# A fused decoder layer on one core: key and value products move to slot 2, the next batch's query product to slot 11

## The reference

```python
def _L0_attn_ref(x, Wq, Wk, Wv):
    q = (x @ Wq.T).reshape(B, S, NH, DK).transpose(0, 2, 1, 3)
    k = x @ Wk.T
    v = x @ Wv.T
    dist = jax.nn.softmax(jnp.einsum('bhqd,bkd->bhqk', q, k) * scale, axis=-1)
    att = jnp.einsum('bhqk,bkd->bhqd', dist, v)
    return att.transpose(0, 2, 1, 3).reshape(B, S, DIM_V)
...
x = _layernorm(x + _L0_attn_ref(x, ...))
x = _layernorm(x + _L0_xattn_ref(x, ctx_1024, ctx_1024, fside_1xSxS2_0, ...))
x = _layernorm(x + _L0_ffn_ref(x, ...))
```

## Time and profile before

| | us |
|---|---|
| median of 3 runs | 1420.98 |
| lowest, highest | 1415.15, 1421.51 |
| the profiled execution, its own time | 1420.46 |
| its span, first to last instruction | 1418.7 |

### The profile page before, as it was taken

How to read it: one execution, slowest core, us unless ns; L and a number is a source line. 1 busy time by engine, 2 the same in 40 slices (tenths; PEclk the granted TensorE clock), 3 DMA queues, 4 the chain that set the end, 5 groups by cost and what they waited for, 6 DMA issues and landing times.

```text
span 1418.7 us, 30148 instructions
## 1 busy us (share of the span) xinstructions
PE 1274.8 (90%) x7734; PEld 900.7 (63%) x7735; DVE 1147.8 (81%) x3145; ACT 747.3 (53%) x1740; POOL 642.5 (45%) x978
## 2 busy tenths in 40 slices
PE   6997999999999999999988569999999999968886
PEld 4443555655556555555553357888888888858886
DVE  0565889898888988988986658888888888869998
ACT  1245777777777787777776212233233223314444
POOL 3011354455444554555445323333333333348886
PEclk9998999999999999999999679999999999989999
DMA  7656667667676675775655853433443344379995
GB/s 163 166 111 125 113 151 172 149 163 149 158 157 140 146 163 135 157 138 145 157 129 195 290 215 129 135 130 129 134 135 129 130 134 135 133 271 330 332 335 194
DMA packets 182817, 237.57 MB, mean 167 GB/s; under 512 B 21376, under 2 KB 144256, under 8 KB 176960
## 3 DMA queue, kind: packets, MB, share of 16 engines
q1 hardware_dynamic: 158864, 169.50, 47.3%
q0 software_dynamic: 17488, 55.02, 10.3%
q10 hardware_dynamic: 6368, 11.89, 2.4%
HBM read 138.34 MB, written 98.30 MB: 167 GB/s over the span
## 4 chain that ended last, share of the span: by engine, by line
PE 62%; DVE 17%; issue 9%; DMA 5%; ACT 4%; POOL 1%; SPq 1%; DVEq 0%; ACTq 0%; POOLq 0%
PE psO L623 6%; PE psS L730 5%; PE psHb L1399 5%; PE psHb L1396 5%; PE psHb L1395 4%; PE psHa L1395 4%; PE psHa L1396 4%; PE psHa L1399 4%; PE psB L652 4%; PE psT L740 4%; DVE negmax L1031 3%; DVE x2in L1591 3%; PE psX L1419 2%; DVE gt_lo L1567 2%; PE psA L612 2%
## 5 line engine op out<-in xcount | busy, mean ns | idle before, releaser
L1031 DVE TENSOR_REDUCE negmax<-psS 128x2 f32<-128x512 f32 x512 | 350.7, 688 | 94.6 <-PE psS L730 77.0
L870 ACT ACTIVATE probs<-psT 128x512 f32<-128x512 f32 x512 | 304.0, 599 | 161.0 <-PE psT L740 143.3
L1476 ACT ACTIVATE sig<-hb 128x512 f32<-128x512 f32 x135 | 85.6, 634 | 286.6 <-DVE hb L1549 286.6
L730 PE MATMUL psS<-kstack,qstack 96*128 96x256 bf16 x1024 | 195.2, 273 | 31.3 <-DVE kstack L1129 15.6
L740 PE MATMUL psT<-qstack,kstack 99*128 99x512 bf16 x512 | 194.8, 383 | 4.4 <-ACT probs L870 4.3
L1358 POOL DMA_INDIRECT g_rows<-g,slot x135 | 134.7, 998 | 69.8 <-issue 66.5
L730 PEld LDWEIGHTS psS<-kstack,qstack 96*128 96x128 bf16 x1024 | 93.1, 104 | 90.2 <-DVE negmax L1031 27.4
L482 POOL DMA_INDIRECT lists<-x,slots x128 | 128.6, 1005 | 33.9 <-issue 30.1
L623 PE MATMUL psO<-probs,vaug 128*32 128x512 f32 x1024 | 139.1, 616 | 0.4 <-ACT probs L870 0.4
L1560 DVE SCALAR_TENSOR_TENSOR g<-g,xe,sig 128x512 f32<-128x512 f32 x135 | 101.5, 752 | 26.0 <-DVE g L1556 16.6
L1549 DVE TENSOR_TENSOR hb<-psHb,b 128x512 f32<-128x512 f32 x135 | 93.4, 692 | 33.1 <-issue 28.9
(11 more groups left out here) (207 smaller groups left out, 2956.4 us busy)
## 6 DMA issues: line engine op xcount, KB each, us to landing
rows<-g_rows SPq DMA_DIRECT2D x32, 1024.0 KB, 8.1
qstack<-q_parts SPq DMA_DIRECT2D x192, 128.0 KB
xe<-lists SPq DMA_DIRECT2D x135, 133.0 KB, 2.1
q_parts<-qpart SPq DMA_DIRECT2D x32, 384.0 KB
sums<-x SPq DMA_DIRECT2D x32, 264.0 KB
x2in<-sums SPq DMA_DIRECT2D x32, 264.0 KB, 4.7
xt<-in_x_t SPq DMA_DIRECT2D x32, 256.0 KB
part_raw<-in_f_t SPq DMA_DIRECT2D x32, 256.0 KB, 5.0
```

Source lines behind the costliest of these rows:

```text
L730: last = mm(psS[:, u % 2, hh * S:(hh + 1) * S], qstack[0:KROWS, b1.s4, 2 * hp + hh, c * P:(c + 1) * P], kstack[0:KROWS, b1.s4, :], start=T ...
L870: nc.scalar.activation(probs[:, u % PT, :], psT[:, u % 2, :], ACT.Exp, scale=SELF_SCALE).then_inc(sm["exp_done"], 1)
L1031: v.tensor_reduce(negmax[:, b1.s2, 2 * hp:2 * hp + 2, c], psS[:, u % 2, :].rearrange("p (h k) -> p h k", h=2), AX.X, ALU.max, negate=True) ...
```

## The change

- PE: the key and value products of batch t move from slot 11 to slot 2. The query product in slot 11 is now that of batch t+1 (`q = t.back(-1)`).
- ACT: the casts of v and k move from slot 12 to 3, the two further k copies from 13 to 5. The cast of q moves from slot 3 to 12.
- DVE: krest moves from slot 12 to 3, k_split from 14 to 7, qrest from 3 to 12.
- POOL: the two instructions that split q leave the step's head and stand at its end, behind `rstd` of the first norm and ahead of the masked bias. Between them no longer stands a wait for `slots_ready`.
- SP: `x_t` is loaded one step earlier. The store of q stands at the head of the step, the six stacking loads ahead of the load of the maxima's rows.
- `bank_b` has q_projected and kv_projected exchanged. `pipeline` begins at n = -1, a step in which only the query product of batch 0 is made.

The diff, cut to its core:

```diff
-        for n in range(B + 7):
+        for n in range(-1, B + 7):
...
-            load_xt(t)
+            load_xt(t.back(-1))
...
+            if active(t):
+                wait(sp, "q1_cast", done(t))
+                wait(sp, "q_split", done(t, 2))
+                sp.dma_start(dram["q"][t.s2].rearrange("t (c p) s -> p t c s", p=P), qpart[:, t.s2]
+                             ).then_inc(sm["q_stored"], 16)
...
+            if active(q):
+                wait(pool, "q_rest", done(q))
+                wait(pool, "q_stored", done(q.back(2), 16))
+                pool.tensor_tensor(qpart[:, q.s2, 1], qrest[:, q.s2], one_c[:, :].unsqueeze(2).to_broadcast([P, DC, S]),
+                                   ALU.mult).then_inc(sm["q_split"], 1)
+                wait(pool, "q_split", 2 * q.n + 1)
+                pool.tensor_tensor(qpart[:, q.s2, 2], qrest[:, q.s2], qpart[:, q.s2, 1], ALU.subtract
+                                   ).then_inc(sm["q_split"], 1)
...
-        bank_b = {"q_projected": ("q_rest", 0, 1, 1), "x2_transposed": ("x2t_copied", 6, 1, 1),
+        bank_b = {"kv_projected": ("k_rest", 0, 1, 1), "x2_transposed": ("x2t_copied", 6, 1, 1),
...
-                  "kv_projected": ("k_rest", 0, 1, 1), "counted": ("slot_link", 6, 3, 1)}
+                  "q_projected": ("q_rest", -1, 1, 1), "counted": ("slot_link", 6, 3, 1)}
...
-                if u == 11 and active(t):
-                    bank_read(bank_b, t, "kv_projected")
...
+                if u == 11 and active(q):
+                    wait(pe, f"xt_loaded{q.s2}", 16 * q.half + 16)
+                    bank_read(bank_b, t, "q_projected")
```

More of the change, by code:

```diff
@@ L388, in step @@
                              ).then_inc(sm[f"ctxv_loaded{b.s2}"], 16)
[L389 to L397, removed]
             b = t
@@ L405, in step @@
                                  ).then_inc(sm[f"q_stacked{b.s2}"], 16)
+            b = t.back(2)
+            if active(b):
+                wait(sp, "m_copied", done(b))
+                sp.dma_start(qstack[KROWS:KROWS + MROWS, b.s4], mrows[:, b.s2]).then_inc(sm[f"m_stacked{b.s2}"], 16)
             store_parts(t)
@@ L506, in step @@
             if active(b7):
-                if not active(t):
-                    wait(pool, "slots_ready", done(b7))
+                wait(pool, "slots_ready", done(b7))
                 dispatch(b7, 0)
@@ L824, in step @@
                     norm(x2, rstd2, shift2, y2, b6, "rstd2_ready", "x2_ready")
+                if u == 5 and active(t):
+                    wait(act, "k_rest", done(t))
+                    copy(kstack[32:64, t.s4], krest[32:64, t.s2])
+                    copy(ksmall[64:80, t.s2], krest[64:80, t.s2]).then_inc(sm["k_mid"], 1)
                 if u == 6 and active(b6) and not draining(t):
@@ L1055, in step @@
                 if u == 3 and active(t):
[L1056 to L1060 removed]
+                    wait(dve, "kv_cast", done(t))
+                    wait(dve, "k_split", done(t.back(2)))
+                    v.tensor_tensor(krest[0:KROWS, t.s2], psB[0:KROWS, 0:S], kstack[0:KROWS, t.s4], ALU.subtract
+                                    ).then_inc(sm["k_rest"], 1)
                 if u == 4 and active(b5):
@@ L1075, in step @@
                                   ).then_inc(sm["gate_link"], 1)
+                if u == 7 and active(t):
+                    wait(dve, "k_mid", done(t))
+                    v.tensor_tensor(kstack[64:80, t.s4], krest[64:80, t.s2], ksmall[64:80, t.s2], ALU.subtract
+                                    ).then_inc(sm["k_split"], 1)
                 if u == 8 and active(b4) and not draining(t):
@@ L1107, in step @@
                                     ).then_inc(sm["hot_ready"], 1)
-                if u == 12 and active(t):
-                    wait(dve, "kv_cast", done(t))
-                    wait(dve, "k_split", done(t.back(2)))
-                    v.tensor_tensor(krest[0:KROWS, t.s2], psB[0:KROWS, 0:S], kstack[0:KROWS, t.s4], ALU.subtract
-                                    ).then_inc(sm["k_rest"], 1)
+                if u == 12 and active(q):
+                    wait(dve, "q1_cast", done(q))
+                    wait(dve, "q_split", done(q.back(2), 2))
+                    v.tensor_tensor(qrest[:, q.s2].rearrange("p c s -> p (c s)"), psB[:, :],
+                                    qpart[:, q.s2, 0].rearrange("p c s -> p (c s)"), ALU.subtract
+                                    ).then_inc(sm["q_rest"], 1)
                 if u == 12 and active(b4) and not draining(t):
@@ L1126, in step @@
                                     ).then_inc(sm["gate_link"], 1)
-                if u == 14 and active(t):
-                    wait(dve, "k_mid", done(t))
-                    v.tensor_tensor(kstack[64:80, t.s4], krest[64:80, t.s2], ksmall[64:80, t.s2], ALU.subtract
-                                    ).then_inc(sm["k_split"], 1)
                 if u == 13 and active(b5):
```

66 lines of the change are left out of this document (25 added, 41 removed).

## The result

| | before | after |
|---|---|---|
| median of the timed runs | 1418.8 us (14 runs) | 1425.8 us (14 runs) |
| range of the runs | 1409.8 to 1423.8 | 1421.8 to 1427.7 |
| profiled execution, its span | 1420.46, 1418.7 | 1426.67, 1424.8 |
| length of a step in the steady part | 21.82 | 22.65 |
| first scores of slot 0 at the border of step 7 | 179.56 | 166.98 |

The changed kernel takes 1.0051 times as long, with a 95% interval of 1.0033 to 1.0069: slower by about 7 us. That is little, but the interval leaves out 1. The forecast was 1432, the range 1403 to 1447.

The account below looks back on a forecast made before the run. PE was taken to set the pace, DVE following closely. 1420.46 - 6.2 (first and last steps) + 25 x 0.70 + 2 x 0.25 = 1432.3, given as 1432 us; range 1403 to 1447.

Parts of the forecast that it names:

- k_split's wait: At the step's head: PE's 0.50 us wait goes, but slot 14's reduction and the first norm come late next.
- The chain to the first norm: Slot 12 on DVE: qrest is 0.26 longer than krest and starts 0.17 later, so rstd, norm and L644 come 0.43 later.
- POOL beside DVE: At the step's end: POOL's q instructions hold the pair's second L1157 for 1.21 us; the second norm comes 0.70 later a step.
- rival M: At the step's end: the second L1157 slips in as well; 0.25 us a step, 1421 us in all; chance 0.25.
- rival X: At the step's end: copy and tensor_scalar wait for POOL too; 1.5 us a step, 1452 us in all; chance 0.14.
- The prediction's own test: In steps 7 to 31 the second L1157 lasts over 1 us if right; L1157 x2 under 0.8 us if wrong.
- G: At the border: the chain to L644 has slack, so the 0.50 wait goes whole; 1401 us in all; chance 0.17.
- The path to x2: From the held pair over L919, POOL's rstd and shift to ACT's second norm, starting at 603.9 in place of 603.20.
- k_split in slot 7: Adds 0.42 us to DVE, where some 2 us of gaps per step were found.
- The first steps: First steps and the last: waits for k_split, x_t and stacked q go, 10.0 us less a 3.8 cost; net 6.2 gained.
- The prediction's own sign: The start is right if PE reaches the border at 135 us some 6 us earlier.
- The 3.8: Step 0: cost of batch 1's added q product, taken between 2.8 (clock rises no later) and 4.7 (clock moves with work).

Follow-up runs that it names:

- experiment 2: Changed kernel with DVE's qrest moved from slot 12 to slot 13, behind the first moments of y1: ratio to before 1.0041, a step of 22.64 us.
- experiment 1: Changed kernel with the tensor_scalar add moved from the step's end to slot 2 of the next step: ratio to before 0.9994, a step of 22.29 us.
- experiment 3: Changed kernel with k_split's subtraction moved from slot 7 to ahead of slot 6's reduction: ratio to before 1.0023, a step of 22.44 us.
- experiment 8: Kernel before with batch 0's query product made once more in step 0, its result unused: ratio to before 0.9979, first scores at 41.42 us.
- experiment 10: Kernel of experiment 4 with the L1157 pair and the copy moved to slot 2 too: ratio to before 0.986, a step of 21.62 us.
- experiment 7: Changed kernel with POOL's q splits back behind the second norm's rstd, and SP's store and stacking back: ratio to before 1.013, a step of 22.83 us.
- experiment 4: Changed kernel with add in slot 2, qrest in slot 13 and k_split in slot 6 together: ratio to before 0.9934, a step of 21.85 us.
- experiment 9: Kernel of experiment 4 with SP's store of q and stacking put back as in the kernel before: ratio to before 0.9923, a step of 21.86 us.

## Why the prediction was right or wrong

**k_split's wait and what is late next: right.** PE's 0.50 went, and the reduction took its place with 0.34 (L728 <- negmax). The chain to the first norm was forecast 0.43 longer; L642 came 0.39 later from the head.

**POOL beside DVE: right in kind and nearly in size, wrong in the instruction.** The forecast had the second L1157 held for 1.21 us, x2's transposes 0.70 later and 22.5 a step. Measured: the pair longer by 0.23, the `tensor_scalar` by 0.96, L918 later by 1.05, x2's transposes by 0.55. The step that failed is the use of the earlier trace rows for a pair of 8 columns. There too the pair starts ahead of the end of POOL's first instruction (1342.36, end 1342.68). But its instructions have 256 columns, and its first one went on to 1342.96, with POOL's second under way since 1342.64:

```profile
1341.39 1.29 POOL L1369 TENSOR_TENSOR row_sum<-rows 128x512 f32<-128x512 f32 x1
...
1342.64 1.47 POOL L1369 TENSOR_TENSOR row_sum<-rows 128x512 f32<-128x512 f32 x1
```

The second L1157 began at 599.89, 0.14 before L518. That is what rival M had said for it, and what followed for the add is rival X's; no rival had both. Experiment 2 let the pair start only as L515 ended, and the forecast hold appeared. The prediction's own test, L1157 over 1 us, would have led to the wrong case, M or G, had one stopped there; the next rows of DVE's queue had to be read.

**The path to x2 had a second branch that was not forecast.** The prediction goes from the hold over L919, `rstd` and shift to the second norm. In the changed kernel a second chain ends at the same norm. ACT and POOL there:

```profile
604.64 0.61 ACT L869 ACTIVATE probs<-psT 128x512 f32<-128x512 f32 x1
604.79 0.20 POOL L473 TENSOR_TENSOR shift<-nmean,rstd 128x2 f32<-128x2 f32 x1
605.13 1.09 ACT L790 ACTIVATE x<-y,shift,rstd 128x256 f32<-128x256 f32 x2
```

The norm starts 0.14 behind the end of shift, but also 0.49 behind the start of the exponential ahead of it on ACT, as it did before, 603.20 behind this:

```profile
602.71 0.62 ACT L870 ACTIVATE probs<-psT 128x512 f32<-128x512 f32 x1
```

That exponential is late by PE's key product, which waited for the bank: 0.39 from the first norm and 0.29 from the bank, less 0.13 between the product and x2's transposes, where the cast of k is shorter than that of q (forecast: up to 0.19), make the 0.55. The forecast chain alone would give nearly the same, 0.53: shift came 1.04 later from the head, it had ended 0.62 ahead of the norm before, and a norm that waits for it starts some 0.11 behind it (597.16 and 597.27). No experiment parts the two; experiment 1 takes both away. The wait at L668, forecast to grow to about 1.5, shrank to 0.73, because PE itself reached it 0.70 later and x2 came 0.55 later.

**Rival X** said that copy and add may be held as well. In experiment 2 the add was, by `mask_b`, for 0.66 behind the 1.27 of the pair; the copy between them was not. X's price of 1.5 a step did not come: the step was 22.64, not 23.3. What the holds cost is what they add to the freeing of the bank, and there the key product followed x1's transposes after 1.66, where 0.93 is what it takes unhindered (experiment 1). The Trainium skill (SBUF — State Buffer, section Who interferes with whom) lets `copy`, `cast` and `tensor_scalar` contend with GpSimd; the trace agrees, with 1.13 for an add and a copy of two columns and 0.63 for the cast L949. The same section says that `tensor_reduce` never contends on trn2. The reduction ran at 0.67 to 0.69 beside POOL's two instructions in every kernel here, but it reads PSUM, so this is no hard test.

**Costed at nothing, wrongly: k_split in slot 7.** The prediction found 2 us of gaps on DVE per step and let 0.42 fall into them. There are two of 0.62 and 0.59 just ahead of slot 7 (at 608.81 and 610.09); from L1076 to `att` there is none, and L609 waited. Experiment 3 puts it at 0.21 of a step, which is most of the 0.29 lost behind slot 5. **The bank of slot 2** was not looked at either: k's product waits for L1168, and starts 0.29 later than L642's delay explains.

**The first steps: half of the gain was missed.** Forecast 10.0 gained less 3.8 for batch 1's q product, net 6.2, of which 5.7 up to step 7; measured 12.6 at the border of step 7. (The prediction's own sign, some 6 us at the border of 134.12, came as 10.5: 123.67.) The 3.8 was the wrong term: it took the added product at the low clock and let the clock rise at the same time as before or later. The clock rose earlier *because* of the work, as experiment 8 shows. First scores came at 42.09 against 44.09, 0.7 of it by an earlier x_t, which is 2.0 gained in place of 3.8 lost. So the gains from there to step 7 are 10.6, close to the forecast 9.5 (10.0 less the 0.5 of the last step). The parts differ, though: the borders into steps 2 and 3 still wait 1.06 each for the reduction, where some 0.5 was taken. A share of these, too, is the clock, which the prediction did not count. PE's windows of before and of after, from the wait of 3.34 on; the columns are length, PE busy, granted clock, DMA share and GB/s:

```profile
112.00:135.00 23.00, 19.05 (x109) 0.88 0.61 120
135.00:160.00 25.00, 23.16 (x144) 0.91 0.59 130
```

```profile
112.00:135.00 23.00, 20.09 (x138) 1.00 0.70 127
135.00:160.00 25.00, 23.21 (x159) 1.00 0.62 116
```

**The sum.** A step costs 0.83 where 0.70 was forecast. Beside its terms: the hold 0.36 (experiment 1; forecast 0.45), k_split 0.21 (experiment 3; forecast nothing), and what is left, 0.26, for the longer chain to the first norm (forecast 0.25). These shares are those of single repairs, and such shares did not add up, so they are no exact account. From the border of step 7 to that of step 31 the changed kernel lost 18.1 (544.59 against 526.49 for 24 steps; 24 times 0.83 would be 19.9, but before had more odd long ones), then 0.6 more: -12.6 + 18.1 + 0.6 = 6.1, the difference of the two spans. The forecast sum is -6.2 + 18.0 = 11.8. (With the 0.5 between profile and median it gives 1433, not 1432.) So the steps were right to 0.7 us, partly by luck, since a step's cost taken too low met fewer regular steps than were counted, and the start was wrong by 6.4, which is nearly all of the 6 us by which the median lies under the forecast. The sign rests on the step.

## What to carry to other kernels

When a large POOL instruction is moved, list every DVE instruction that reads only SBUF within its whole time, copies and adds of two columns too. Price one hold for whichever comes there, and follow it to everything behind it in DVE's queue, a freed bank as well as the statistics. Better, give these small ones a slot in which POOL is silent, as experiments 1 and 10 did for 0.36 and 0.23 us a step. Of gaps "somewhere in the step" only those count that lie between the moved instruction and the next thing waited for. And test repairs together: three that gave 0.36, 0.01 and 0.21 alone gave 0.80.

## What the runs showed of the hardware that was not expected

- An add or a copy of 2 columns is held as long as the POOL instruction lasts: 1.13 us in place of 0.16. Which one of a row of small instructions is held changed with a shift of 0.43 us.
- A small POOL instruction held nothing. In the changed kernel L471 (128x2, the power) ran from 604.02 to 604.72, and DVE's L948, with two SBUF inputs of 32 columns, took 0.18 from 604.21 on. Beside POOL's L496 of 512 columns the same instruction (there L947) took 0.99 (experiment 7).
- One more query product in step 0 made PE finish sooner, 41.3 and 41.4 against 44.1 us, 0.8 and 0.65 of it by an earlier x_t, the rest as the full clock was granted earlier. The reverse was seen at waits of 1.98, 2.47 and 3.34 us for the stacked q: the eight matmuls with V behind the wait (L620, L623) took 1.92, 1.94 and 1.59 in place of 1.06. Such a wait costs more than its length.
- The last steps differ between executions by some 2 to 3 us, and the granted clock with them: by 3.1 between the kernels of experiments 4 and 9, whose last steps have the same work, and by 1.6 between the two profiles of experiment 8's one kernel. That is as much as a late stacking costs at the start. What a change at one place gives is read there, not in the total.
